# Queries and keys normalised ahead of a lot's routing in VectorE's attention step

## The reference

```python
x = x + 0.5 * ffn(layernorm(x))
x = x + attn(layernorm(x))
x = x + 0.5 * ffn(layernorm(x))

# ffn: a router picks one of 8 experts for each token
logits = xf @ Wr.T + br
expert_idx = argmax(logits, axis=-1)
out = (relu(xf @ W1[e].T + b1[e]) @ W2[e].T + b2[e])   # e = the token's expert

# attn: 16 heads of 8 features
q, k = rope(rms(q)), rope(rms(k))          # rms: g * t * rsqrt(mean(t*t) + EPS)
attn = softmax(q @ k.T / sqrt(8) + 1.0)
y = (attn @ v) @ wproj.T
```

## Time and profile before

| | |
|---|---|
| Median of 3 runs | 493.08 us (492.8 to 496.94) |
| Profiled execution | 493.35 us, of which the span from the first to the last instruction is 491.5 us |
| TensorE | 433.9 us busy, 88% of the span; mean granted clock 0.951 |
| VectorE | 380.5 us busy, 77% |
| GpSimd | 358.6 us busy, 73% |
| ScalarE | 349.3 us busy, 71% |

### The profile page before, as it was taken

One profiled execution on the slowest core, in us unless ns is written; L12 is line 12 of the kernel. 1 busy time (PEld: TensorE's weight loads), 2 busy tenths in 40 slices (PEclk: granted clock), 3 DMA queues, 4 the chain that ended last, 5 costly groups with the idle time before them and its releaser, 6 DMA issues.

```text
span 491.5 us, 14012 instructions
## 1 busy us (share of the span) xinstructions
PE 433.9 (88%) x4108; PEld 322.8 (66%) x4108; DVE 380.5 (77%) x1037; ACT 349.3 (71%) x782; POOL 358.6 (73%) x579
## 2 busy tenths in 40 slices
PE   7998999969888989999999998988797979799994
PEld 4348998758665555656566655665464459789994
DVE  4785788758787788898988889888788647777772
ACT  4316776757745789999999898888666856557671
POOL 8028898999968588878684874399747616889985
PEclk9798999989997899999999999999899889999998
DMA  7962335251100000000000000000001123223210
GB/s 196 275 255 51 92 89 150 61 164 37 35 24 16 8 25 15 13 8 8 14 14 2 3 3 3 2 13 17 22 25 35 35 57 79 67 84 90 69 37 6
DMA packets 28649, 27.02 MB, mean 55 GB/s; under 512 B 5684, under 2 KB 25947, under 8 KB 28018
## 3 DMA queue, kind: packets, MB, share of 16 engines
q1 hardware_dynamic: 24034, 17.65, 12.1%
q0 software_dynamic: 4544, 8.49, 6.3%
HBM read 16.56 MB, written 12.71 MB: 60 GB/s over the span
## 4 chain that ended last, share of the span: by engine, by line
PE 39%; DVE 19%; POOL 18%; issue 13%; ACT 7%; DMA 1%; DVEq 1%; SPq 1%; ACTq 1%; POOLq 1%
DVE Smax L1732 8%; PE PS L1001 7%; PE PS L860 7%; PE PS L876 6%; PE PS L954 5%; POOL out L629 5%; PE PS L977 4%; POOL Unread L600 4%; PE PS L936 3%; DVE St L1375 2%; ACT Pt L1218 2%; PE PS L920 2%; POOL Pt L607 2%; POOL XX L638 1%; ACT QkT L1122 1%
## 5 line engine op out<-in xcount | busy, mean ns | idle before, releaser
L1732 DVE TENSOR_REDUCE Smax<-PS 128x4 f32<-128x1024 f32 x128 | 155.7, 1223 | 36.3 <-PE PS L954 35.5
L1218 ACT ACTIVATE Pt<-PS 128x1024 f32<-128x1024 f32 x128 | 126.4, 1024 | 20.2 <-PE PS L977 16.9
L876 PE MATMUL PS<-W,HsT 128*128 x624 | 87.4, 284 | 5.7 <-ACT HsT L1163 2.0
L860 PE MATMUL PS<-XsT,Ws 128*128 128x128 f32 x624 | 85.6, 282 | 2.4 <-ACT XsT L1122 2.0
L876 PEld LDWEIGHTS PS<-W,HsT 128*128 128x128 f32 x624 | 77.7, 196 | 10.5 <-issue 9.1
L860 PEld LDWEIGHTS PS<-XsT,Ws 128*128 128x128 f32 x624 | 79.0, 197 | 5.3 <-ACT XsT L1122 2.6
L1001 PE MATMUL PS<-Pt,Vg 128*32 128x256 f32 x1024 | 72.8, 404 | 0.2
L703 POOL TENSOR_TENSOR HL<-Rn,Zero 128x512 fp32r<-128x512 f32 x28 | 35.3, 1282 | 41.8 <-DVE Rn L1715 40.3
L954 PE MATMUL PS<-QkT 24*128 24x256 f32 x512 | 61.3, 312 | 3.0 <-DVE Smax L1732 2.0
L600 POOL MEMSET Unread<- 128x352 f32 (+1 forms) x140 | 62.0, 443 | 0.1
L607 POOL DMA_INDIRECT Pt<-rows,TokI x39 | 40.6, 1040 | 28.6 <-DVE TokI L1573 20.4
(11 more groups left out here) (251 smaller groups left out, 726.4 us busy)
## 6 DMA issues: line engine op xcount, KB each, us to landing
AtCol<-slots SPq DMA_DIRECT2D x39, 65.5 KB, 1.8
rows<-XX SPq DMA_DIRECT2D x8, 288.0 KB, 4.3
XX<-x SPq DMA_DIRECT2D x8, 256.0 KB, 5.1
W<-w1T SPq DMA_DIRECT2D x2, 1024.0 KB, 6.1
W<-w2T SPq DMA_DIRECT2D x2, 1024.0 KB, 9.3
mid<-mid_second SPq DMA_DIRECT2D x1, 1472.0 KB
mid<-Ys SPq DMA_DIRECT2D x16, 64.0 KB
QkT<-NmaxT SPq DMA_DIRECT2D x64, 4.0 KB
```

The source lines that it names most:

```text
L860: last = nc.tensor.matmul(PS[:, h_bank(n) + c // 2, (c % 2) * P:(c % 2 + 1) * P], Ws[:, n % R_WS, c * P:(c + 1) * P], XsT[:, n % 2, :], st ...
L876: last = nc.tensor.matmul(PS[:, y_bank(n), 0:P], HsT[:, n % 2, c, :], W2[:, ds(e * D_FF + c * P, P)], start=(c == 0), stop=(c == FC - 1))
L1218: nc.scalar.activation(Pt[:, m % 2, 2 * pair:2 * pair + 2, :, :].rearrange("p h c t -> p (h c t)"), PS[:, score_bank(m, pair):score_bank(m ...
L1732: nc.vector.tensor_reduce(Smax[:, b % 2, :, at:at + 33:32].rearrange("p t h -> p h t"), PS[:, max_bank(m, pair):max_bank(m, pair) + 2, :]. ...
```

## The change

In VectorE's `step(n)` the two lines that call `normalise` stand behind `sums` and ahead of `lot_place`; before, they stood behind `lot_seen`.

```diff
                 if seq(n, 13) >= 0:
                     sums(seq(n, 13))
+                if norm_seq(n) >= 0:
+                    normalise(norm_seq(n))
                 if n in PLACE_AT:
                     lot_place(PLACE_AT[n])
                 if n in NORM_AT:
...
                 if n in SEEN_AT:
                     lot_seen(SEEN_AT[n])
-                if norm_seq(n) >= 0:
-                    normalise(norm_seq(n))
                 if n == TABLE_AT:
                     full_table()
```

## The result

| | before | changed |
|---|---|---|
| median of 4 runs each | 492.94 us | 508.79 us |
| lowest to highest | 492.69 to 496.94 | 506.44 to 514.61 |
| profiled execution (span) | 493.35 (491.5) | 506.44 (504.6) |
| mean granted clock of the profiled execution | 0.951 | 0.940 |

The ratio is 1.0336 with a 95% interval from 1.0275 to 1.0398: slower by 3.4%. On the 493.08 us that the prediction started from, that is 509.7 us.

The account below looks back on a forecast made before the run. Bound taken: the chain from VectorE's maxima to TensorE's transposes, without slack. 3.7 + 1.8 + 3.3 - 0.7 + 2.7 = +10.8 us on 493.35 gave 504.15, less 0.27 for the median: 503.9 us, range 495.5 to 509.

Parts of the forecast that it names:

- The path: Around steps 38, 42 and 50: VectorE's delay ahead of the maxima passes to TensorE's transposes one for one, without slack.
- The earlier split: After step 42 GpSimd's chain starts 1.1 us earlier, removing VectorE's 0.68 us wait in step 49: gain 0.7 us.
- The collision: Routing on VectorE beside GpSimd's split waits for its instructions: +3.7, +1.8, +3.3 us in steps 38, 42, 50.
- Two instructions per turn: Forecast case: two VectorE instructions pass between GpSimd's in the three steps; total 503.9 us, chance 0.55.
- Nothing is held: Rival: no stalls in the three steps, only step 49's gain of 0.7 us: 492.4 us, chance 0.12.
- only a few instructions wait: Rival: scans or the conversion are exempt from waiting in the three steps: 495.4 to 501.1 us, chance 0.15.
- One instruction per turn: Rival: one VectorE instruction passes per GpSimd turn; stalls +5.2, +2.6, +3.5 us, total 506.4 to 509.1, chance 0.15.
- The change does not do what it says: Rival: something else holds Rn at its new place, so the time stays at 493.1 us; chance 0.03.
- the clock term: One added stretch of TensorE at 1.2 GHz after step 38's idle time: +2.7 us; step 50 has its own already.
- The base: The terms were added to the profiled execution's 493.35 us, then 0.27 taken off for the median.

Follow-up runs that it names:

- run 4: Changed kernel with `normalise` at its new place only in step 42 and at its old place otherwise: 493.11 us, 1.0019 of before.
- Run 1: Changed kernel with GpSimd's splits of sequences 12, 13 and 15 also waiting for the routing: 493.26 us, 1.0011 of before.
- run 2: Changed kernel with GpSimd's splits of sequences 12, 13 and 15 replaced by memsets of a tile nobody reads: 487.76 us, 0.992 of before.
- Run 3: Changed kernel with matmuls of no use on TensorE in steps 39 (15), 43 (6) and 51 (13): 498.22 us, 1.0063 of before.
- Run 8: Kernel before with lot 1's routing moved to steps that have no `normalise`: 489.43 us, 0.9934 of before.
- run 5: Changed kernel with `normalise` at its new place only in step 38 and at its old place otherwise: 494.4 us, 1.0096 of before.
- run 9: Kernel before with matmuls of no use on TensorE in steps 50 (4), 51 (2) and 52 (2): 490.81 us, 0.9929 of before.

## Why the prediction was right in its direction and too small

- **The path.** VectorE to the maxima to TensorE without slack: right, by the chain and by the 8.3 us more of idle time ahead of L936.
- **The earlier split.** 0.7 us in step 49 forecast, 0.68 found; run 4 shows that it comes from step 42.
- **The collision.** Two instructions per turn gave +3.7, +1.8 and +3.3; found were 3.67, 1.62 and 3.10. Run 1 shows that the meeting makes them, run 2 that a GpSimd which only writes doesn't. The scans' lengths are those of the turn that I took; only in the gap ahead of L710 did a third or, in step 50, a fourth one pass (1099, 154, 153, 153, 691, 154, 687, 154 ns). The Trainium skill's page "SBUF — State Buffer", section "SBUF: two separate sides", says that the pair of ports is held for the whole instruction; the trace agrees (the scan from 299.70 ends 0.04 us behind the L703 that held it).
- **The rivals.** "Nothing is held" and "only a few instructions wait" fall with L1426, the scans and L1451. "One instruction per turn" gave a total of 506.4 to 509.1, close to the measured 508.8, but from stalls of 5.2 in step 38 which aren't there; it was near for a wrong reason. "The change does not do what it says" falls with Rn, which runs ahead of the routing in all three steps.
- **The step that failed** is the clock term: "In step 38 TensorE will stand idle for over 4 us, longer than there, so I add one such stretch: +2.7." I counted one added stretch of the size of the earlier trace rows, and took step 50's as already paid for by the kernel before. The price of one stretch was right: 2.48 and 2.54 us were found behind steps 38 and 42. Their number and length were not: both steps brought one, and the one behind step 50 grew from 6.8 to 20.5 us. Instead of 2.7 the clock cost 8.4 us from step 39 to `experts(1)` in the profiled pair and some 6.5 over all executions. Run 3 gets this back without touching a stall (mean clock 0.967, level +8.4), which shows that it is the clock.
- **The base.** The sum was built on one profiled execution, but the clock differs from execution to execution, ahead of step 38 too. The profiled pair differs there by -3.19 us, where both kernels run the same instructions, and the changed kernel's profiled execution was the fastest of its four. So the pair shows +13.1 us where the medians show +15.8.

Open: what decides whether a low stretch comes and how long it lasts. Run 8 had one of 17 us behind 0.99 us of idle time, run 5's profile lacked the one that the kernel before has at 351 us, and the clock parts of the single steps don't sum to that of the whole.

## What to carry to other kernels

Before an instruction that releases GpSimd is moved ahead, look at what VectorE then does beside it: two-input operations on SBUF, scans and conversions wait for whole GpSimd tensor operations, and a row of tiny ones loses a turn at every second one: here 0.75 us of scans became 3.27. Time in which GpSimd merely waits for VectorE can be what keeps the two apart. A stall that idles TensorE can then be paid for almost twice, since the clock may fall behind it: here 6.5 us of clock came on top of 8.4 us of stalls, though steps 38 and 42 alone cost no net clock. Price it from all stretches of several executions, not from one stretch of one profile, and try matmuls of no use in the gap.

## What I had not expected of the hardware

- A granted clock of 0.50 can last over 20 us with TensorE busy for 18.04 of 20.5 us (88%), and it moves a kernel whose program is unchanged between 485.33 us (mean clock 0.980) and 495.8 (0.944).
- Eight matmuls of no use gained 0.7% on the kernel before (run 9), though at one clock it costs 0.9 us more with them.
- One copy on VectorE was held by GpSimd's memset (0.17 to 0.34 us in run 2), while a scan and a two-input operation beside it were not.
